# A scan step's preparation placed four half tiles earlier

## The reference, cut to what matters

```
xi, z = split(x @ in_proj_w.T); xc = silu(depthwise_conv3x3(xi) + conv_b)       # D = 192 channels
xs    = 4 orders of the 4096 pixels (K = 4)
dts, Bs, Cs = split(einsum('bkdl,kcd->bkcl', xs, x_proj_w), [6, 22])            # rank 6, N = 16 states
delta = softplus(einsum('bkrl,kdr->bkdl', dts, dt_w) + dt_b);  A = -exp(A_logs)
h[t]  = exp(delta[t] * A) * h[t-1] + (delta[t] * u[t]) * B[t]                   # for all 4096 t
y[t]  = sum_n h[t] * C[t] + Ds * u[t]
out   = (layernorm(sum of the 4 orders back in image order) * silu(z)) @ out_proj_w.T
```

## Time and profile before

| | us |
|---|---|
| median of 3 runs | 11442.28 (11442.05 to 11461.41) |
| profiled execution | 11436.57 |
| its span | 11434.8 |
| VectorE busy in the span | 10175.8 (89%) |
| GpSimd | 9743.0 (85%) |
| TensorE (matmul) | 8854.3 (77%) |
| ScalarE | 6998.9 (61%) |
| mean granted TensorE clock | 0.737 of full |

### The profile page before, as it was taken

The page is one execution under the profiler, slowest core; times in us unless marked ns, Lnnn a source line. Parts: engine busy times, 40 slices in busy tenths (PEclk is TensorE's granted clock), DMA queues, the critical chain, the costliest instruction groups (busy, mean ns, idle before and its releaser), DMA issues.

```text
span 11434.8 us, 94421 instructions
## 1 busy us (share of the span) xinstructions
PE 8854.3 (77%) x26272; PEld 2214.9 (19%) x26272; DVE 10175.8 (89%) x6087; ACT 6998.9 (61%) x10714; POOL 9743.0 (85%) x4231
## 2 busy tenths in 40 slices
PE   7876688876879677879777788888688877787757
PEld 2211111211112111212112121122111221122213
DVE  4999998999899999989999899899988999999873
ACT  5655555665556555677566765566755666667654
POOL 4899998899888999888988888888988889998860
PEclk8865577865779567769677787788677876777766
DMA  4666688576875566556776668856687566665550
GB/s 113 145 148 136 128 167 157 140 147 135 163 153 140 141 150 168 144 128 144 170 154 155 132 141 171 151 141 138 140 163 148 139 148 140 154 161 125 122 136 17
DMA packets 1779114, 1627.02 MB, mean 142 GB/s; under 512 B 1323598, under 2 KB 1324912, under 8 KB 1778588
## 3 DMA queue, kind: packets, MB, share of 16 engines
q1 hardware_dynamic: 1778588, 1620.97, 64.5%
HBM read 623.22 MB, written 192.15 MB: 71 GB/s over the span
## 4 chain that ended last, share of the span: by engine, by line
DVE 20%; PE 18%; issue 17%; POOL 15%; ACT 7%; SPq 3%; DMA 3%; DVEq 0%; POOLq 0%; ACTq 0%
POOL pr L1676 10%; DVE hs L1570 8%; DVE ps L1555 7%; DVE hs L1566 4%; PE ps L898 3%; PE ps L1068 3%; PE ps L1055 2%; PE ps L863 2%; PE ps L1046 2%; POOL dur L1690 2%; ACT dec L1319 1%; POOL bup L1690 1%; POOL us L1667 1%; PE ps L1030 1%; SPq L754 1%
## 5 line engine op out<-in xcount | busy, mean ns | idle before, releaser
L1676 POOL TENSOR_TENSOR pr<-hs,crep 128x1024 f32<-128x1024 f32 x3072 | 7190.8, 2357 | 1174.0 <-PE ps L1068 566.6
L1570 DVE TENSOR_TENSOR_SCAN hs<-dec,carry,ps 128x1024 f32<-128x1024 f32 x1728 | 4053.5, 2346 | 233.8 <-POOL pr L1676 9.8
L1055 PE MATMUL ps<-sbc,selb 96*128 96x512 bf16 x4608 | 1845.3, 493 | 1783.4 <-DVE hs L1570 1255.7
L1555 DVE TENSOR_TENSOR ps<-ps,dur 128x1024 f32<-128x1024 f32 x2304 | 2787.9, 1210 | 485.8 <-PE ps L1055 375.3
L1319 ACT ACTIVATE dec<-dtr,ac 128x1024 f32<-128x1024 f32 x2304 | 2610.6, 1136 | 433.2 <-DVE hs L1570 422.5
L1068 PE MATMUL ps<-pr,red 128*32 128x512 f32 x12288 | 2281.6, 825 | 30.6 <-POOL pr L1676 22.6
L1326 ACT ACTIVATE carry<-hs 128x1 f32<-128x1 f32 x2304 | 457.1, 199 | 2420.8 <-DVE hs L1570 2240.9
L1570 DVE TENSOR_TENSOR_SCAN hs<-dec,zero,ps 128x1024 f32<-128x1024 f32 x576 | 1351.1, 2346 | 72.8 <-ACT dec L1319 1.7
L863 PE MATMUL ps<-xb,tapw 96*96 96x512 f32 x2304 | 1189.5, 637 | 51.4 <-ACT sd L1152 48.9
L1055 PEld LDWEIGHTS ps<-sbc,selb 96*128 96x128 bf16 x4608 | 379.2, 108 | 3922.2 <-DVE hs L1570 2340.8
L1319 ACT ACTIVATE ps<-dtr,ac 128x1024 f32<-128x1024 f32 x768 | 848.1, 1105 | 398.8 <-DVE hs L1570 398.8
(11 more groups left out here) (228 smaller groups left out, 7601.2 us busy)
## 6 DMA issues: line engine op xcount, KB each, us to landing
dtr<-de SPq DMA_DIRECT2D x768, 512.0 KB, 8.1
dur<-us SPq DMA_DIRECT2D x768, 512.0 KB, 8.6
crep<-bc_d SPq DMA_DIRECT2D x512, 512.0 KB, 6.6
ust<-u_d SPq DMA_DIRECT2D x256, 384.0 KB, 5.9
y_d<-yst SPq DMA_DIRECT2D x768, 128.0 KB, 3.4
sd<-y_d SPq DMA_DIRECT2D x448, 192.0 KB, 5.1
brep<-bc_d SPq DMA_DIRECT2D x128, 512.0 KB, 5.7
u_d<-sd SPq DMA_DIRECT2D x64, 384.0 KB, 3.2
```

Source lines behind the costliest of these rows:

```text
L1055: mm = pe.matmul(ps[:, SLOT + 2 * (n % RS) + hf, :], selb[:, i % GT // 2, :], sbc[:, w % 2, B * hf:B * (hf + 1)], start=True, stop=True)
L1555: dve.tensor_tensor(slot(n), slot(n), dur[:, 2 * (G % 2) + i % 2, :], ALU.mult).then_inc(bu_v, 1)
L1570: dve.tensor_tensor_scan(hs[:, n % RH, :], dec[:, others(n) % RD, :], slot(n), init, ALU.mult, ALU.add).then_inc(scan_v, 1)
L1676: pool.tensor_tensor(pr[:, n % RP, :], hs[:, n % RH, :], crep[:, q, :], ALU.mult).then_inc(prod_g, 1)
```

## The change

The first two numbers and the last two go down by 4: gathers from -10 to -14, the first half's chain from -6 to -10, the second half's from 14 to 10, softplus from 33 to 29. The loop ahead of step 0 that runs the negative places of step 1 starts at -14 on both engines. `late` steps and step 0 keep their places; SP, GpSimd and VectorE have no edit.

```diff
@@ prep_places
-    return (8, 11, 2, 21, 33) if late(w) else (-10, -6, 4, 14, 33)
+    return (8, 11, 2, 21, 33) if late(w) else (-14, -10, 4, 10, 29)
@@ tensor
-            for place in range(-10, 0):
+            for place in range(-14, 0):
                 prepare_at(place, 1)
```

## The result

The changed kernel takes 11522.17 us (median of 4 runs, 11507.11 to 11534.13) against 11451.52 (4 runs, 11442.05 to 11461.41): ratio 1.0066, 95% interval 1.0054 to 1.0079. It is slower by 0.66%, where the forecast was 11450 with 11396 to 11508. The profiled execution took 11507.11 us, its span is 11505.3, 70.5 us more than before. By the ends of the scans 58.7 of the 70.5 lie in steps 1 to 127, 3.5 in step 0, and 8.3 behind the last scan. That last stretch takes 376 us in the profiled execution of before and 375 in that of e8, and 383 to 386 in all the others, also in e6 and e7 with the places of before; so the 8.3 us are not the change's.

A forecast was written before the change was run, and what follows sets the result against it. The scan loop was taken to run at VectorE's pace. TensorE's minus 10 and ScalarE's plus 18 gave plus 8 us on 11436.6, and with 5.7 us for the median 11450 us; 8 in 10 was 11396 to 11508.

The forecast's parts named there:

- ScalarE: plus 18 us: Net cost on ScalarE of moving the softplus block to tile 14, ahead of tile 17's decay: 18 us.
- Scans late for a decay: Scans waiting where side work lies in tiles 13 to 16: 25 us, less 5 for scan 19's waits.
- Evictions behind the block hold up repetition 17, 6 steps of about 2 us, 12: Side-work evictions falling into the softplus block delay TensorE's repetition of B for tile 17: 12 us.
- Feed-forward keeps out of the block, minus 14: Feed-forward evictions were to avoid the moved softplus block as before, and some product 20 waits to go: minus 14 us.
- Slower: Rival: softplus ahead of two short tiles costs half of 98 busy steps 1.2 us each; 11505 us, chance 0.32.
- faster rival: Rival: most costs on TensorE stay covered, 78 us gained, 10 lost there, 18 on ScalarE; 11392 us, chance 0.26.
- TensorE: minus 10 us: Moved projections and size passes on TensorE: 78 us gained at products, 68 us of costs, net minus 10 us.
- tile 19: Gets the first projection; product 21 was to wait longer, 15 times 2 us, 30 us.
- tile 5: Gets the second projection in place of a size pass; product 8 was to pay 25 times 0.7 us, 17.
- tile 11: Gets a size pass for a residue; with tile 1, 35 places at 0.6 us, 21 us.
- Rest, 0 of 0 to 20 us: Moved gathers, first split and store of C and B: bounds 0 to 20 us, taken as 0 because covered.
- What would show it: The prediction's list of signs: waits of products 8, 9, 17, 21, late decays, quiet step at 78.3 us, total near 375.

The follow-up runs named there:

- e8: The changed kernel with softplus at half tile 35 instead of 29: 11546.07 us, ratio 1.0084 to the kernel before.
- e6: The kernel before with one load of y issued a half tile earlier, in place 1: 11441.59 us, ratio 0.9994 to the kernel before.
- e7: The kernel before with softplus at half tile 35 instead of 33: 11469.19 us, ratio 1.0014 to the kernel before.
- e1: The changed kernel with softplus back at half tile 33, chains and gathers still moved: 11449.83 us, ratio 1.0003 to the kernel before.
- e9: The changed kernel with softplus as ln(1 + exp(x)), no table load, in one piece at 29: 11504.49 us, ratio 1.0065 to the kernel before.
- e3: The changed kernel with softplus at half tile 31 instead of 29: 11489.35 us, ratio 1.0030 to the kernel before.
- e12: The changed kernel with one load of y issued a half tile earlier, in place 1: 11491.80 us, ratio 1.0044 to the kernel before.
- e10: The changed kernel with softplus as ln(1 + exp(x)), one half at 29 and one at 31: 11466.78 us, ratio 1.0033 to the kernel before.
- e4: The changed kernel with 12 added zero-weight matmuls ahead of TensorE's wait for y, in place 1: 11533.52 us, ratio 1.0071 to the kernel before.
- e5: The changed kernel with softplus at 33 and one load of y a half tile earlier, in place 1: 11403.82 us, ratio 0.9964 to the kernel before.
- e11: The changed kernel with the earlier load of y and softplus in two parts at 31 and 33: 11381.95 us, ratio 0.9954 to the kernel before.

## Why the prediction was wrong

The failed step is the size of **ScalarE: plus 18 us**. e1 against after gives the moved block 0.63%, 72 us, four times that. The prediction had the block and its neighbours right, and left out or priced too low what stands behind it in ScalarE's queue. By its terms:
- *Scans late for a decay*, 25 less 5: measured 8.5 to 36.0 us, plus 28, in tiles 17 and 18 as foretold, and 19 fell from 6.2 to 1.6. Close in the sum; tile 17 is late in 19 steps, most of them by under 1 us, three by 2.5 to 4.2.
- *Evictions behind the block hold up repetition 17, 6 steps of about 2 us, 12*: ten steps, 54.2 us. The mechanism was named and its price was wrong. I took a delay over the old place, and the rows of steps 37 and 58 show the whole of it: 5.77 and 6.95 us of TensorE's idle time, because the evictions come behind the block, in step 58 also behind a decay and each other, and repetition 17 behind them.
- *Feed-forward keeps out of the block, minus 14*: not there against before, where product 20 went from 18.1 to 16.3 us. Four of the ten waits lie in steps with attention and feed-forward beside them (57, 58, 121, 122), and places 9 and 10 together went from 1188.6 to 1214.7 us. Against e1, which has the first chain at its new place and the block still at 33, products 20 and 21 do fall, by 32 us.
- Not in the sum at all: VectorE's own layer norm waits for ScalarE (L1467), plus 20 us.

From e1 to after, the traces have plus 53 us at product 17, plus 31 at scans 17 and 18, plus 16 at L1467 and minus 32 at products 20 and 21. These two profiled executions are only 37 us apart, since e1's is the longest of its ten and that of after the shortest of its four, so the 72 us of the medians can't be split up in full.

The **Slower** rival had the right mechanism, the block ahead of the short tiles, and its 11505 us is near 11522 (its own terms, 11450 and 49 times 1.2, make 11509), but it spread the price over half of the busy steps at 1.2 us. The trace has most of it in few steps at 2.8 to 6.2 us. Nor was its reason the right one: with 98 busy steps, the scan of tile 17 was late in 19 and product 17 in 13. A fixed piece of 4.8 us stood ahead of results for which two other engines wait in order. e9 shows that the table loads in it don't matter. So the 11505 is in part luck, and it stood inside the range, while the faster rival's 11392 lay outside it. On the drain of 1.38 us at a switch, which the Trainium skill (ScalarE: Activation LUTs, What ACT_TABLE_LOAD costs) states, the rows after agree with those before: the load takes 1.28 us and the next activation begins 0.02 us behind it. The rows were the right guide there. (That section prices a switch; it has no word on a softplus.)

**TensorE: minus 10 us.** e1 has this term alone: 1.0003 (0.9990 to 1.0015), plus 3 us on the median with minus 11 to plus 17. As a sum it held, in part by luck, since larger costs and larger gains than foretold stood against each other. Gains in e1: product 9 39.7 to 20.6 (foretold minus 33), product 17 34.9 to 6.1 (minus 22), product 0 78.8 to 56.4 (minus 13; the prediction's 81.6 holds two waits for a load of `dur` besides). Costs: tile 19 plus 34 at products 20 and 21 (30, though it was the block at 33 that made them; after, with it at 29, they rose by 2 us), tile 5 plus 13 at product 8 (17). The part that failed inside is tile 11: I priced a size pass at 0.6 us; products 12 and 13 pay 39 us, 34 of them in seven steps of place 1, where a load of y had been hidden by slow tiles ahead of it. That no load was touched didn't mean that none could become late.

**Rest, 0 of 0 to 20 us.** The gathers keep their cover where the softplus stands clear of them: nothing in e1 points at them. With the block beside them, in e8, the loss is 0.84%; it is not the case of the change itself.

**What would show it.** Product 9 to a third: it fell to 0.41. Product 17 to a third: it rose to 1.7 times, the clearest refutation. Products 8 and 21 up by 17 and 30: by 6 and 4. Decays late in tiles 17 and 18 and not in 19: right. Quiet steps 78.3: right; so that test of the slower rival let it pass, since the loss is in the busy steps alone. Total of product waits near 375: 399, and no measure, as e1 shows.

Open: why e3 and after keep different waits in single steps, what TensorE's clock alone costs in place 1, whether the load and the block depend on each other (e12), and whether it is the cut or the later place that helps in e10.

## What to carry to other kernels

Price a long unbroken piece on an in-order engine by what stands behind it in the queue, the evictions on which another engine waits before its own critical work, and not only by its nearest consumer; if it must be in a tight place, try it cut into parts with the critical operation between them, and measure the later place of the last part by itself (here the cut with its second part at 31 cost 0.33% and the whole block at 31 0.30%). When a step gets faster, look for the transfer that its slowness had covered: the gain shows only once that load is issued earlier (here 1.0003 became 0.9964). Move one thing at a time when several can be separated, since the chains' move was neutral and the softplus that travelled with them cost it all.

## What the runs showed of the hardware

- TensorE's granted clock fell to 1.2 GHz behind 2.79 us of back-to-back bf16 matmuls and 2.5 us of an idle time of 2.57 (e4, step 33: 1.00 during the matmuls, 0.50 from 2952.38 on, passes of 1.01 us). Before, in the same step, an idle time of 2.76 us was followed by passes of 0.55 us at 1.00, and the clock fell to 0.50 only at 2924.07, 1.3 us behind the wait. The length of the idle time alone doesn't tell which it will be.
- A softplus with two table loads (4.8 us) and one of four activations without (4.5 us) cost the same time in the kernel, 1.0066 and 1.0065.
- TensorE's busy time isn't a constant of the work: 8854 us before, 8813.5 in e5 and 8796.2 in e11 with the same 26272 matmuls, at mean granted clocks of 0.737, 0.746 and 0.748. The mean clock alone doesn't give it: e1 has 8875.3 us at 0.741.
